# Layer 1's attention as one run of 48 steps instead of six rounds of eight: sums in two PSUM banks, one eviction to a step

## The reference

```python
x_tokens = xh.transpose(0, 2, 1).reshape(bsz, C_head)
...
q_vec = _layernorm(zq @ q_proj_w.T + q_proj_b, ln_gamma, ln_beta)
k_vec = _layernorm(zk @ k_proj_w.T + k_proj_b, ln_gamma, ln_beta)
...
scores = -(qn + kn - 2.0 * qk) / tau
attn = jax.nn.softmax(scores, axis=-1)
v = xh.transpose(0, 2, 1)
out = jnp.einsum('bst,btc->bsc', attn, v)
out = attn_gate * out.transpose(0, 2, 1)
return out.reshape(B, C, H, W)
```

## Time and profile before

| | us |
|---|---|
| Time, median of three runs | 8861.34 (8860.65 to 8866.9) |
| The profiled execution: span, first to last instruction | 8833.4 |
| Median less that span | 27.9 |
| PE busy in the span | 7445.8 (84%) |
| DVE / ACT / POOL busy | 5679.0 / 3844.7 / 2220.5 |
| Sixteen attention windows, together | 1700.3 |

### The profile page before, as it was taken

How to read it: one execution, slowest core, us unless ns; L and a number is a source line. 1 busy time by engine, 2 the same in 40 slices (tenths; PEclk the granted TensorE clock), 3 DMA queues, 4 the chain that set the end, 5 groups by cost and what they waited for, 6 DMA issues and landing times.

```text
span 8833.4 us, 95654 instructions
## 1 busy us (share of the span) xinstructions
PE 7445.8 (84%) x35246; PEld 3495.5 (40%) x35246; DVE 5679.0 (64%) x9661; ACT 3844.7 (44%) x7430; POOL 2220.5 (25%) x1862
## 2 busy tenths in 40 slices
PE   7989889989989995668888888888888888888867
PEld 4544444445544452123333333333333333333343
DVE  4666656566665663457667667766766766766674
ACT  4444444444544552443543543444354354354330
POOL 1222222222222220012421421331231232133152
PEclk9999999999999996679899889899888888888988
DMA  1111111111111112024444544554444454354375
GB/s 64 35 38 37 36 37 38 40 38 44 42 42 38 41 38 72 4 78 118 153 141 107 169 150 112 149 163 116 133 152 129 117 160 144 97 167 146 99 220 145
DMA packets 244211, 849.75 MB, mean 96 GB/s; under 512 B 46413, under 2 KB 49177, under 8 KB 243361
## 3 DMA queue, kind: packets, MB, share of 16 engines
q1 hardware_dynamic: 150272, 388.71, 16.4%
q0 software_dynamic: 92160, 453.06, 16.2%
q10 hardware_dynamic: 1312, 1.87, 0.1%
HBM read 602.10 MB, written 89.68 MB: 78 GB/s over the span
## 4 chain that ended last, share of the span: by engine, by line
PE 39%; DVE 13%; ACT 6%; DMA 3%; issue 3%; SPq 2%; POOL 1%; DVEq 0%; ACTq 0%; POOLq 0%
PE ps L2189 10%; PE ps L2649 4%; PE ps L2434 4%; DVE arena L1901 4%; PE ps L2199 3%; PE ps L2660 2%; PE ps L2630 2%; PE ps L2127 2%; PE ps L2320 2%; SPq L2683 2%; PE ps L2113 2%; DMA arena<-arena 1%; DVE arena L400 1%; DMA arena<-img,arena 1%; PE ps L2152 1%
## 5 line engine op out<-in xcount | busy, mean ns | idle before, releaser
L2467 POOL DMA_INDIRECT arena<-img,arena x1152 | 1369.8, 1189 | 2685.6 <-DMA img<-arena 1859.8
L2364 DVE SCALAR_TENSOR_TENSOR arena<-arena 128x384 f32<-128x384 f32 x1152 | 748.0, 649 | 656.6 <-DMA arena<-img,arena 653.6
L1901 DVE TENSOR_REDUCE arena<-ps 128x2 f32<-128x1024 f32 x768 | 894.3, 1216 | 322.6 <-PE ps L2168 319.6
L2042 ACT ACTIVATE arena<-ps 128x512 f32<-128x512 f32 x1536 | 817.5, 603 | 315.1 <-PE ps L2199 312.4
L2189 PE MATMUL ps<-arena 128*64 128x512 f32 x3072 | 935.7, 711 | 0.0
L982 POOL TENSOR_TENSOR arena<-arena 128x512 f32<-128x512 f32 x384 | 442.1, 1158 | 1942.5 <-DMA arena<-decay 1942.4
L2649 PE MATMUL ps<-arena 128*64 128x512 f32 x3072 | 808.1, 651 | 129.6 <-DMA arena<-arena 73.9
L2434 PEld LDWEIGHTS ps<-arena 128*96 128x96 f32 x4608 | 557.9, 174 | 202.1 <-issue 201.7
L2434 PE MATMUL ps<-arena 128*96 128x128 f32 x4608 | 610.4, 289 | 26.3 <-DVE arena L2353 26.2
L1115 DVE TENSOR_TENSOR arena<-ps,arena 128x512 f32<-128x512 f32 x384 | 265.4, 691 | 492.3 <-issue 270.5
L949 PE MATMUL ps<-arena 128*128 128x512 f32 x1152 | 507.2, 596 | 0.0
(11 more groups left out here) (344 smaller groups left out, 12092.7 us busy)
## 6 DMA issues: line engine op xcount, KB each, us to landing
arena<-arena SPq DMA_DIRECT2D x1024, 144.5 KB, 2.9
arena<-decay SPq DMA_DIRECT2D x384, 256.0 KB, 3.2
img<-arena SPq DMA_DIRECT2D x162, 384.0 KB, 2.6
arena<-img,arena POOLq DMA_INDIRECT x1152, 4.5
arena<-y SPq DMA_DIRECT2D x16, 768.0 KB, 6.4
arena<-x SPq DMA_DIRECT2D x16, 768.0 KB, 6.3
out<-arena SPq DMA_DIRECT2D x16, 768.0 KB
arena<-x SPq DMA_DIRECT2D x16, 512.0 KB, 5.1
```

The source lines that it names most:

```text
L1901: dve.tensor_reduce(out, self.wides[B.at("max", b, g, n, h) // 2].rearrange("p (a b) -> p a b", a=2), AX.X, AL.max).then_inc(*S.mark("max_ ...
L2042: act.activation(self.p[n % 6], B("score", b, n)[:, :], ACT.Exp).then_inc(*S.mark("p_act", b, n))
L2364: dve.scalar_tensor_tensor(gb[:, 0:384], gb[:, 384:768], pp[:, 1, n:n + 1], gb[:, 0:384], AL.mult, AL.add).then_inc(*S.mark("corner_x", b, n))
L2467: pool.indirect_dma_start(self.g[n % 6], None, img, bass.IndirectOffsetOnAxis(ap=ii[:, n:n + 1], axis=0)).then_inc(*S.landed(f"{self.tag}g ...
```

## The change

The six rounds become one loop over t = 0..53, eight steps a round and no ninth. At step t PE issues the scores of step t (while t < 48) and the products of step t - 2, across the rounds' borders. Scores use banks 0 to 2 (`n % 3`), sums banks 3 and 4 in turn. ACT does the exps of step t and, in four of every eight steps from step 10 on, one of the four evictions of a round; `finish(0)` moves to step 38 on ACT and 39 on DVE, `act_affine` to 40, `dve_add` to 44 (before: 36, 36, 36 and 42). The tables in `PACE` are as they were, so the second stream's steps stand at the same numbers, but the first stream's work under those numbers is another.

```diff
--- before.py
+++ after.py
@@ -154,6 +154,9 @@
             i = self.i
             self.i = (i + 1) % len(self.t)
         self.held.add(i)
+        return self._use(i, key, by)
+
+    def on(self, i, key, by):
         return self._use(i, key, by)
 
     def pair(self, key, by):
@@ -1921,12 +1924,12 @@
 
         yield from maxima(0)
         yield from maxima(1)
-        yield from skip(18)
-        yield from skip(18)
-        finish(0)
-        yield from skip(6)
-        self.dve_add(dve, b + 1)
-        yield from skip(12)
+        for t in range(54):
+            if t == 39:
+                finish(0)
+            if t == 44:
+                self.dve_add(dve, b + 1)
+            yield
         finish(1)
 
     def act(self, act, b):
@@ -2031,36 +2034,37 @@
             yield from split(fq[:, g, :], 0, g, (2, g))
             yield
 
-        def attend(p):
-            for h in range(2):
-                for tb in range(8):
-                    for m in range(2):
-                        n = 32 * p + 16 * h + 2 * tb + m
-                        act.wait_ge(*S("score_pe", b, n))
-                        act.wait_ge(*S("pv1_pe", b, n - 6))
-                        act.table(ACT.Exp)
-                        act.activation(self.p[n % 6], B("score", b, n)[:, :], ACT.Exp).then_inc(*S.mark("p_act", b, n))
-                    yield
-                o = B("out1", b, p, h)
-                act.wait_ge(*S("pv1_pe", b, 32 * p + 16 * h + 15))
-                for m in range(2):
-                    g, j = (2 * p + m) // 3, (2 * p + m) % 3
-                    act.activation(self.nf[g][32 * j:32 * j + 32, H(h)], o[64 * m + 32:64 * m + 64, :], ACT.Ln).then_inc(*S.mark("att_act", b, "ln", p, h, m))
-                    act.activation(fq[32 * j:32 * j + 32, g, H(h)], o[64 * m:64 * m + 32, :], ACT.Copy).then_inc(*S.mark("att_act", b, "num", p, h, m))
-                yield
+        def evict(n, m, den):
+            p, h = divmod(n, 2)
+            g, j = divmod(2 * p + m, 3)
+            o = B("out1", b, n)
+            act.wait_ge(*S("pv1_pe", b, 16 * n + 15))
+            if den:
+                act.activation(self.nf[g][32 * j:32 * j + 32, H(h)], o[64 * m + 32:64 * m + 64, :], ACT.Ln).then_inc(*S.mark("att_act", b, "ln", n, m))
+            else:
+                act.activation(fq[32 * j:32 * j + 32, g, H(h)], o[64 * m:64 * m + 32, :], ACT.Copy).then_inc(*S.mark("att_act", b, "num", n, m))
 
         def finish(g):
             nf = self.nf[g]
-            act.wait_ge(*S("att_act", b, "num", 1 + g, 1, 1))
+            act.wait_ge(*S("att_act", b, "num", 3 + 2 * g, 1))
             act.activation(nf, nf, ACT.Exp, scale=-1.0).then_inc(*S.mark("att_act", b, "inv", g))
 
         yield from maxima(0)
         yield from maxima(1)
-        yield from attend(0)
-        yield from attend(1)
-        finish(0)
-        self.act_affine(act, b + 1)
-        yield from attend(2)
+        for t in range(54):
+            for n in range(2 * t, min(2 * t + 2, 96)):
+                act.wait_ge(*S("score_pe", b, n))
+                act.wait_ge(*S("pv1_pe", b, n - 6))
+                act.table(ACT.Exp)
+                act.activation(self.p[n % 6], B("score", b, n)[:, :], ACT.Exp).then_inc(*S.mark("p_act", b, n))
+            n, k = divmod(t - 10, 8)
+            if n >= 0 and k < 4:
+                evict(n, k // 2, k % 2 == 0)
+            if t == 38:
+                finish(0)
+            if t == 40:
+                self.act_affine(act, b + 1)
+            yield
         finish(1)
 
     def pe(self, pe, b):
@@ -2177,40 +2181,35 @@
                 i.then_inc(*S.mark("mt_pe", b, g, h))
             yield from skip(4)
 
-        def attend(p):
-            for h in range(2):
-                o, free = B.hold(("out1", b, p, h), ("att_act", b, "num", p, h, 1), 4)
+        def score(t):
+            p, h, tb = t // 16, t // 8 % 2, t % 8
+            for n in range(2 * t, 2 * t + 2):
+                g, j = divmod(2 * p + n % 2, 3)
+                r = slice(32 * j, 32 * j + 32)
+                ps, free = B.on(n % 3, ("score", b, n), ("p_act", b, n))
                 pe.wait_ge(*free)
-
-                def back(n):
-                    tb, m = n % 16 // 2, n % 2
-                    hd = 2 * p + m
-                    pe.wait_ge(*S("p_act", b, n))
-                    pe.matmul(o[64 * m:64 * m + 64, :], self.va[:, tb, 64 * hd:64 * hd + 64], self.p[n % 6], start=tb == 0, stop=tb == 7).then_inc(*S.mark("pv1_pe", b, n))
-
-                n0 = 32 * p + 16 * h
-                for tb in range(8):
-                    for m in range(2):
-                        n, hd = n0 + 2 * tb + m, 2 * p + m
-                        ps, free = B.take(("score", b, n), ("p_act", b, n))
-                        pe.wait_ge(*free)
-                        pe.wait_ge(*S("split_dve", b, 2, hd // 3, 1))
-                        r = slice(32 * (hd % 3), 32 * (hd % 3) + 32)
-                        pe.matmul(ps[:, :], ks[r, hd // 3, 128 * tb:128 * tb + 128], qs[r, hd // 3, H(h)], start=True, stop=True).then_inc(*S.mark("score_pe", b, n))
-                    if tb > 1:
-                        back(n - 5)
-                        back(n - 4)
-                    yield
-                for n in range(n0 + 12, n0 + 16):
-                    back(n)
-                B.drop(("out1", b, p, h))
-                yield
+                pe.wait_ge(*S("split_dve", b, 2, g, 1))
+                pe.matmul(ps[:, :], ks[r, g, 128 * tb:128 * tb + 128], qs[r, g, H(h)], start=True, stop=True).then_inc(*S.mark("score_pe", b, n))
+
+        def back(t):
+            p, tb = t // 16, t % 8
+            if tb == 0:
+                _, free = B.on(3 + t // 8 % 2, ("out1", b, t // 8), ("att_act", b, "num", t // 8, 1))
+                pe.wait_ge(*free)
+            o = B("out1", b, t // 8)
+            for m in range(2):
+                n, hd = 2 * t + m, 2 * p + m
+                pe.wait_ge(*S("p_act", b, n))
+                pe.matmul(o[64 * m:64 * m + 64, :], self.va[:, tb, 64 * hd:64 * hd + 64], self.p[n % 6], start=tb == 0, stop=tb == 7).then_inc(*S.mark("pv1_pe", b, n))
 
         yield from maxima(0)
         yield from maxima(1)
-        yield from attend(0)
-        yield from attend(1)
-        yield from attend(2)
+        for t in range(54):
+            if t < 48:
+                score(t)
+            if 2 <= t < 50:
+                back(t - 2)
+            yield
 
     def sp(self, sp, b):
         yield from skip(32 + 10 + 16)
```

## The result

The changed kernel takes **8753.8 us** (median of four runs, 8743.8 to 8764.8), the kernel before in the same session 8864.0; ratio 0.9877, 95% interval 0.9862 to 0.9893. Forecast were 8711 and a range of 8620 to 8820. So 110 us came where 150 were expected.

A forecast was written before the change was run, and what follows sets the result against it. PE, busy 84%, was taken as the bound. Shorter windows (119 us for images 1 to 14, 22 first, 9 last) total 150; span 8833.4 becomes 8683, plus 27.9 around it gives 8711 us; range 8620 to 8820.

The forecast's parts named there:

- Borders: Five round borders an image lose their four products in a row and the waits for last exps and evictions.
- Start: Start of an image's attention: 2.4 us idle and 4.6 lost to half clock stay; L2418's 1.93 us wait goes.
- third score bank: Scores in three banks: each waits for the previous step's first exp, 0.25 us to spare, cost 0.
- Evictions: One eviction a step makes ACT late: 0.8 us of PE idleness a round without second-stream matmuls beside it.
- finish(0) and affine: On ACT, steps 38 and 40: 3.4 us of PE idleness, then 5 us at half clock, 2.3 lost.
- rival 1: ACT's lateness is partly absorbed and the affine gap brings no half clock: 8648 us, chance 0.20.
- Clock: PE's granted clock in the attention windows rises to about 0.92; image 5 still loses 4.6 and 2.3 us.
- Rival 3: Many short gaps hold TensorE at half clock, 45 us a window instead of 15: 8926 us, chance 0.09.
- The step that failed: DVE: finish(0) behind `weigh` of chunk 2 helps L2434; later chunks used 16 us apart, DVE needs 11.6; wait nothing.
- the prediction's own sign of being wrong: Listed as showing the forecast wrong: L2434 waiting for `weigh` by more than a microsecond a chunk.
- rival 2: Gathers, corners and `weigh` set the pace, PE waits at L2434, images gain 2 to 4 us: 8795 us, chance 0.13.
- The 6.12 us at L435 unchanged: PE's idleness from the last product over evictions, finish(1) and group norm to L435 stays 6.12 us.

The follow-up runs named there:

- a0: The change again, unedited, on chip 7: 9016 us, 1.0007 of the kernel before.
- e8: The change with gathers of an eighth of the bytes, on chip 5: 8710 us, 0.9831 of the kernel before.
- a1: The change a third time, unedited, on chip 3: 8746 us, 0.9879 of the kernel before.
- e6: The kernel before with scores in three banks instead of four, on chip 7: 9061 us, 1.0062 of the kernel before.
- e4: The change with `dve_add` at step 46 instead of 44, on chip 7: 9009 us, 0.9997 of the kernel before.
- e9: The change with evictions every other step, ACT's finish(0) at 40, affine at 41, DVE's finish(0) and dve_add at 46, chip 3: 8696 us, 0.9821.
- e0: The kernel before, unchanged, run again on chip 4: 9014 us, 1.0005 of the kernel before.

## Why the prediction was right, and where its sum was off

- **Borders: right.** 104.1 to 80.1 us in image 0 (82 forecast), and 78.9 to 79.6 in a0, e8 and a1, on chips 7, 5 and 3; image 5 96.1 (97.6). No score waits for an eviction any more.
- **Start: right.** The 2.4 us are still there, and the 1.93 at L2418 are gone (in the sixteen windows such waits fell from 33.1 to 7.4 us). Only the third score bank, put at nothing, costs 0.5 us and more an image here (e6).
- **Evictions: 1.03 us a bare round, not 0.8.** ACT (exps, eviction, exps, eviction, in a bare round):

```profile
5204.07 1.09 ACT L2059 ACTIVATE arena<-ps 128x512 f32<-128x512 f32 x2 [0.24 <-PE ps L2192]
5205.18 0.59 ACT L2043 ACTIVATE arena<-ps 32x512 f32<-32x512 f32 x1
5205.79 1.09 ACT L2059 ACTIVATE arena<-ps 128x512 f32<-128x512 f32 x2
5206.90 0.59 ACT L2045 ACTIVATE arena<-ps 32x512 f32<-32x512 f32 x1
```

  A step with an eviction takes ACT 1.72 us, not 1.60: an exp overlaps the next exp, but an eviction overlaps neither neighbour (1.11 and 0.61 between starts, 1.09 and 0.59 of work). The Trainium skill (ScalarE: Activation LUTs, What ACT_TABLE_LOAD costs), with its overlap of about 93 ns, would have given 0.4, an estimate; two exps agree with it (0.59 us each, 0.49 apart), evictions do not, and the measurement decides. Of the 1.03 little is counted as idle: PE's scores last up to 0.79 instead of 0.39 us.
- **finish(0) and affine: 3.4 + 2.3 forecast, about 2.7 found** in image 5 (steps 38 to 42, against 1.33 each), with no half clock behind them; in image 0 of a0 and e4 there was some (2.2 and 2.1 us for the two steps behind). That the gap brings no half clock is what rival 1 said.
- **Clock: right.** PEclk 0.95 in image 5's window (about 0.92 forecast), half clock for 10 us an image where it was 27. Rival 3's swinging clock did not come. Its support was also weaker than stated: the rows of image 0's maxima show the clock at 0.50 throughout, and no swing between two levels.
- **Windows in all: 150 forecast, 168 found.** 9.1 us in each of images 2 to 14 (8.5 forecast), 24 in image 0 (22), 16.5 in the last (9). Of the last one's, 4.2 are no gain: its window now ends at step 49, and 36 matmuls of L2434 stand behind it (144 of them inside, 180 before).
- **The step that failed: DVE.** "finish(0) moves behind `weigh` of chunk 2, which helps L2434", and later chunks are used 16 us apart against 11.6 of DVE's work. Both halves were wrong at chunk 3. DVE: left out were `finish(0)`, `dve_add` and their waits for ACT, which now all lie between `weigh(2)` and `weigh(3)`, 9.6 us in a row, and some 5 us of waiting for gathers; it is 25.0 us and not 11.6. PE: chunk 3 has no nine steps ahead of it, since the change leaves nothing on PE in steps 50 to 53; it is 10.1 us and not 16. The wait, put at nothing, is 68 us at this chunk, 4.3 an image, where the prediction's own sign of being wrong was 1 us a chunk. With some 2.1 us of half clock an image behind it, less 32 us that PE now waits less at the group norm (145.2 against 176.8), it makes up the 58 us given back. It is rival 2's mechanism, but at chunk 3, not at chunk 0, whose spare of 2.4 us held (no wait at all). e9 undoes most of it.
- **How near the number came is in part luck.** 110 us of 150 came, 43 us above the forecast. The windows gave more than the whole forecast, and that covered part of a wait that the sum did not have.
- **"The 6.12 us at L435 unchanged": wrong.** It is 3.6, with a wait of 4.8 and 2.1 of half clock ahead of it; together 4.7 us more an image (8.9 to 13.6).
- **Around the span lie 1.8 us, not 27.9.** The profiled execution of the kernel before was some 26 us faster than its median. The difference of 150 was in effect taken from the median, so this did not move the forecast.
- **The chance of no change, 0.04**, knew nothing of late signals. The gain came in the first pair (0.9877), on chip 3 (0.9879) and, with thin gathers, on chip 5 (0.9845). On chips 4 and 7 neither the change nor a variant of it gained anything.

## To carry to other kernels

When a stretch of the bound engine is shortened, list for each engine that feeds its next wait all that lies between two of its deliveries, waits included: what was moved "out of the way" of one delivery stands in the way of the next. Read the mechanism in a piece that nothing disturbs (here image 0), and the gain in the whole. A pipeline in which every step waits for a signal of the step before has no slack for a late one: measure such a change on more than one chip.

## Of the hardware, unexpected

- On chips 4 and 7 signals from PE to ACT came up to 15 us late (e4), for 117 to 145 exps an execution, nearly all beside gathers and none in image 0; beside the first pair's the kernel before took 150 us more and the change 260. On the others not one was late. POOL's gathers last as long on both sorts (mean 1.19 us in the first execution of the kernel before, and in e0). In all eight executions with late signals the 16 DMA engines were at least 0.68 busy in the 4 us ahead of every late score (median 0.86 to 0.88, added up from the traces' DMA packets). A busy share alone does not bring it: in e0 119 other exps that waited had 0.75 or more ahead of them and were in time, and in the first execution of the kernel before all 264 such. Whether bytes, landings or something outside the core makes them late stays open: the thin gathers ran on a chip without them.
- A gather that starts while DVE runs without a pause can be held until DVE's next one (3.98 and 8.77 us instead of 0.95).
